# Two Mamba layers of 32 units each: two phases with their own set-up, or one phase of 64 units

## The reference, cut to what matters

```python
def _mamba_block(seq, ln_g, ln_b, in_w, conv_w, conv_b, xproj_w, dt_w, dt_b, A_log, Dp, out_w):
    h = (seq - mu) * jax.lax.rsqrt(var + EPS) * ln_g + ln_b          # over the 96 channels
    xs, z = jnp.split(h @ in_w, 2, axis=-1)                          # 192 each
    xc = silu(sum(conv_w[:, k] * xp[:, k:k + L, :] for k in range(4)) + conv_b)   # causal
    dbl = xc @ xproj_w                                               # 6 + 16 + 16
    delta = softplus(dbl[..., :6] @ dt_w + dt_b)
    dA = exp(delta[..., None] * A)                                   # A = -exp(A_log), 192 x 16
    dBx = delta[..., None] * Bm[:, :, None, :] * xc[..., None]
    hstates = scan of h[l] = dA[l] * h[l-1] + dBx[l]                 # l = 0 .. 4095
    y = (einsum('blds,bls->bld', hstates, Cm) + Dp * xc) * silu(z)
    return y @ out_w

for i in range(2):                                                   # the two layers
    seq = seq + _mamba_block(seq, <weights of layer i>)
```

## Time and profile before

| | |
|---|---|
| median of 3 runs | 7883.33 us (7870.8 to 7883.77) |
| the profiled execution | 7886.06 us, its span 7884.2 us |
| TensorE's granted clock, mean of full speed | 0.865 |
| busy share of the span: DVE, PE, POOL, ACT | 82%, 79%, 69%, 67% |
| `mamba_hs` scans on DVE, both layers | 1536, of 1271 ns mean |
| `mamba_prod` on POOL, both layers | 1536, 1929.6 us |
| Mamba layers, from the first instruction to the fusion's first one on DVE | about 3119 us |

### The profile page before, as it was taken

How to read it: one execution, slowest core, us unless ns; L and a number is a source line. 1 busy time by engine, 2 the same in 40 slices (tenths; PEclk the granted TensorE clock), 3 DMA queues, 4 the chain that set the end, 5 groups by cost and what they waited for, 6 DMA issues and landing times. The chain is left out here.

```text
span 7884.2 us, 105029 instructions
## 1 busy us (share of the span) xinstructions
PE 6253.2 (79%) x18336; PEld 2158.2 (27%) x18336; DVE 6471.5 (82%) x7496; ACT 5278.1 (67%) x10931; POOL 5467.5 (69%) x4288
## 2 busy tenths in 40 slices
PE   7888788678888885477888888888888777889786
PEld 2222222122222221122222222222222212478342
DVE  6999999869999998379999999999999995633636
ACT  6777777667777774366777777777777774322656
POOL 5888888768888886068888888888888893000516
PEclk8888988889888887688888999888888887998888
DMA  3444444344444444367777777777777774246322
GB/s 91 105 98 96 104 105 103 77 94 97 99 109 104 98 99 107 109 162 176 174 181 180 180 181 180 180 179 183 180 179 181 182 184 105 92 155 178 103 65 74
DMA packets 580429, 1050.78 MB, mean 133 GB/s; under 512 B 101719, under 2 KB 136812, under 8 KB 575180
## 3 DMA queue, kind: packets, MB, share of 16 engines
q1 hardware_dynamic: 580140, 1047.89, 54.7%
HBM read 858.09 MB, written 189.54 MB: 133 GB/s over the span
## 5 line engine op out<-in xcount | busy, mean ns | idle before, releaser
L1574 POOL TENSOR_TENSOR scan_prod<-scan_hs,scan_BC_rep 128x512 f32<-128x512 f32 x1536 | 1942.9, 1274 | 427.5 <-DVE scan_hs L1498 422.8
L597 POOL TENSOR_TENSOR mamba_prod<-mamba_hs,mamba_BC_rep 128x512 f32<-128x512 f32 x1536 | 1929.6, 1273 | 387.4 <-DVE mamba_hs L557 365.2
L557 DVE TENSOR_TENSOR_SCAN mamba_hs<-mamba_dA,mamba_carry,mamba_dbx 128x512 f32<-128x512 f32 x1152 | 1463.9, 1271 | 0.0
L1123 PE MATMUL scan_u_rep<-scan_du,scan_sel 96*128 96x512 f32 x1536 | 968.7, 716 | 472.4 <-DVE scan_hs L1498 471.8
L496 ACT ACTIVATE mamba_dA<-mamba_delta_rep,mamba_a_neg 128x512 f32<-128x512 f32 x1536 | 1091.0, 712 | 202.2 <-DVE mamba_hs L557 201.2
L1348 ACT ACTIVATE scan_dA<-scan_delta_rep,scan_a_neg 128x512 f32<-128x512 f32 x1536 | 1092.3, 712 | 90.9 <-DVE scan_hs L1498 80.4
L1498 DVE TENSOR_TENSOR_SCAN scan_hs<-scan_dA,scan_carry,scan_u_rep 128x512 f32<-128x512 f32 x768 | 976.0, 1271 | 158.6 <-ACT scan_carry L1328 153.9
L544 DVE TENSOR_TENSOR mamba_dbx<-mamba_u_rep,mamba_BC_rep 128x512 f32<-128x512 f32 x1152 | 788.0, 684 | 309.4 <-DMA mamba_BC_rep<-bc_units 131.9
L1498 DVE TENSOR_TENSOR_SCAN scan_hs<-scan_dA,scan_carry,scan_dbx_even 128x512 f32<-128x512 f32 x768 | 975.5, 1270 | 31.7 <-ACT scan_carry L1328 27.3
L315 PE MATMUL mamba_u_rep<-mamba_du,mamba_sel 96*128 96x512 f32 x768 | 483.4, 715 | 406.8 <-DVE mamba_hs L557 400.1
L1897 POOL TENSOR_TENSOR ffn_sq<-ffn_xm 96x512 f32<-96x512 f32 x64 | 66.3, 1036 | 954.7 <-DVE ffn_xm L1865 944.6
(11 more groups left out here) (283 smaller groups left out, 10476.9 us busy)
## 6 DMA issues: line engine op xcount, KB each, us to landing
scan_BC_rep<-proj_rows SPq DMA_DIRECT2D x1024, 256.0 KB, 6.4
scan_delta_rep<-proj_rows SPq DMA_DIRECT2D x1024, 192.0 KB, 3.5
mamba_BC_rep<-bc_units SPq DMA_DIRECT2D x256, 512.0 KB, 10.4
mamba_delta_rep<-delta_units SPq DMA_DIRECT2D x512, 192.0 KB, 3.6
proj_rows<-scan_dbc SPq DMA_DIRECT2D x256, 224.0 KB, 2.6
delta_units<-mamba_delta SPq DMA_DIRECT2D x128, 192.0 KB, 6.2
by_n<-fin_res SPq DMA_DIRECT2D x32, 768.0 KB, 3.2
fmid_src<-by_n SPq DMA_DIRECT2D x32, 768.0 KB, 5.0
```

Of the source, the lines that this page charges most:

```text
L557: nc.vector.tensor_tensor_scan(hs[:, s % RING_H], dA[:, s % RING_A], dbx_bank(s)[:], carry[:, bass.ds(at, 1)], op0=ALU.mult, op1=ALU.add). ...
L597: pool.tensor_tensor(prod[:, (G * u + s) % RING_P], hs[:, s % RING_H], BC_rep[:, u, QUADS + s % QUADS], ALU.mult).then_inc(s_prod, 1)
L1123: nc.tensor.matmul(u_rep[c][:], sel[:, c], du[:, k], start=True, stop=True).then_inc(s_rep_u, 1)
L1574: pool.tensor_tensor(prod[:, (G * k + s) % RING_P], hs[:, (G * k + s) % RING_H], BC_rep[:, k, 2 + s % 2], ALU.mult).then_inc(s_prod, 1)
```

## The change

`mamba_phase` is called once, with three arrays (`x_units`, `seq[0]`, `seq[1]`) and both layers' weights. Its units are numbered 0 to 63; unit 32 is the second layer's first. `bodies` now gives each unit the layers of the units from n - 1 to n + 3, and has two loops of 13 pairs (2 to 27 and 34 to 59) with straight code around: 0 and 1, 28 to 33, and 60 to 63. All steps take their weights from the layer of the unit they work on, so that units 30 and 31 prepare units 32 and 33 with layer 1's weights.

- Weights stand twice, as lists by layer. To save space the taps are loaded into `w_conv` and multiplied in place, A_log into `a_neg`, and the small `x_dt` and `w_dt` into rows of `hs`. Both sets are loaded at the start, the second right after the first two inputs; ACT and PE derive the second set after they have prepared unit 1, and DVE its taps before its first product.
- `carry` is a ring of 8 unit slots (and a ninth that takes what the first layer's last four units hand on, which nobody reads). At unit 28 DVE waits for its own last scan and clears the four slots in which units 32 to 35 begin.
- Units are loaded from and stored to the array of their layer.
- The barrier and the set-up between the layers are gone.

What it does to the order on the engines:

DVE, the kernel before, from the last scans of the first layer to the first product of the second (L525 to L534 set up constants and the taps).

The diff, cut to its core (every `lay` that is only passed on is left out):

```diff
-def mamba_phase(nc, name, x_in, x_out, bc_rows, delta_rows, w):
+def mamba_phase(nc, name, x_layers, bc_rows, delta_rows, weights):
...
+    NU = 2 * UNITS
+    SLOTS = 2 * B
...
+        w_in, w_conv, conv_b, dt_b, skip, ln_g, ln_b, w_proj, w_out, a_neg, skip_w = (
+            [p.sb(f"{what}{lay}", shape) for lay in range(2)]
...
+        x_dt, w_dt = ([hs[0:R, 2 * lay + v, 0:2 * C] for lay in range(2)] for v in range(2))
...
-        carry = p.sb("carry", [128, (UNITS + B) * G])
+        carry = p.sb("carry", [128, (SLOTS + 1) * G])
...
+            def at(n):
+                body(n, n % 2, [m // UNITS if 0 <= m < NU else None for m in (n - 1, n, n + 1, n + 2, n + 3)])
+
+            for n in range(2):
+                at(n)
+            for first, end, lay in ((2, UNITS - 4, 0), (UNITS + 2, NU - 4, 1)):
+                with eng.Fori(first // 2, end // 2) as i:
+                    body(2 * i, 0, [lay] * 5)
+                    body(2 * i + 1, 1, [lay] * 5)
+                for n in range(end, min(end + 6, NU)):
+                    at(n)
...
+            load_weights(0, s_w, ((sel, "sel"), (gather, "gather"), (ident, "ident")))
+            x_first = x_layers[0]
+            sp.dma_start(xin[:, 0], x_first[:, 0]).then_inc(s_xin[0], 16)
+            sp.dma_start(xin[:, 1], x_first[:, 1]).then_inc(s_xin[1], 16)
+            load_weights(1, s_w1, ())
...
+            pe.wait_ge(s_w1, 16 * NW1)
+            delta_weights(1)
+            pe.wait_ge(s_wconv1, 1)
+            pe.wait_ge(s_wd, 4)
+            pe.wait_ge(s_diag, 5)
             pe.wait_ge(s_du, 1)
...
+            def layer_weights(lay):
+                nc.scalar.activation(a_neg[lay][:], a_neg[lay][:], ACT.Exp).then_inc(s_aexp, 1)
+                act.wait_ge(s_aexp, lay + 1)
+                nc.scalar.mul(a_neg[lay][:], a_neg[lay][:], -1.0).then_inc(s_a, 1)
...
+            act.wait_ge(s_w1, 16 * NW1)
+            layer_weights(1)
             bodies(act, body)
...
+            conv_weights(0, s_wconv)
+            dve.wait_ge(s_w1, 16 * NW1)
+            conv_weights(1, s_wconv1)
...
+                at_first, = (dve.snap(v) for v in (n % SLOTS * G,))
+                if isinstance(n, int) and n == UNITS - B:
+                    dve.wait_ge(s_scan, G * n)
+                    nc.vector.memset(carry[:, UNITS % SLOTS * G:(UNITS % SLOTS + B) * G], 0.0).then_inc(s_zeroed, 1)
+                if isinstance(n, int) and n == UNITS:
+                    dve.wait_ge(s_zeroed, 1)
...
-                    at = G * n + s
+                    at = at_first + s
...
-    mamba_phase(nc, "mamba0", x_units, seq[0], bc_units, delta_units, w["mamba0"])
-    mamba_phase(nc, "mamba1", seq[0], seq[1], bc_units, delta_units, w["mamba1"])
+    mamba_phase(nc, "mamba", (x_units, *seq), bc_units, delta_units, (w["mamba0"], w["mamba1"]))
```

More of the change, by code:

```diff
@@ L225, in spread, with body @@
                 spread_delta(v, 1, landed)
-            def body(n, u, has_next, has_ahead):
-                load, last, read, done, landed = (sp.snap(v) for v in (n + 3, n - 1, n + 2, n + 2, 16 * n + 32))
-                now = sp.snap(n)
-                if not (isinstance(n, int) and n + 3 >= UNITS):
+            def body(n, u, lays):
+                prev, lay, nxt, _, after = lays
+                read, done, landed, now = (sp.snap(v) for v in (n + 2, n + 2, 16 * n + 32, n))
+                own, = (sp.snap(v) for v in (n - UNITS * lay,))
+                if after is not None:
+                    load = sp.snap(n + 3 - UNITS * after)
@@ L232, in body @@
                     wait(sp, s_mean, read)
-                    sp.dma_start(xin[:, 1 - u], x_in[:, bass.ds(load, 1)].rearrange("c a t -> c (a t)")
+                    sp.dma_start(xin[:, 1 - u], x_layers[after][:, bass.ds(load, 1)].rearrange("c a t -> c (a t)")
                                  ).then_inc(s_xin[1 - u], 16)
-                wait(sp, s_out, last)
-                sp.dma_start(xres[:, u], x_in[:, bass.ds(now, 1)].rearrange("c a t -> c (a t)")
+                if prev is not None:
+                    sp.wait_ge(s_out, now)
@@ L256, in _, with delta_weights @@
             pe.wait_ge(s_w, 16 * NW)
-            for half in range(2):
-                if half:
-                    pe.wait_ge(s_wd, 1)
-                nc.tensor.matmul(y[:, 0:2 * C], x_dt[:, half * C:half * C + C], w_dt[:],
-                                 start=True, stop=True).then_inc(s_wd_ps, 1)
-            pe.wait_ge(s_set, 4)
+            def delta_weights(lay):
+                for half in range(2):
+                    wait(pe, s_wd, 2 * lay + half)
+                    nc.tensor.matmul(y[:, 0:2 * C], x_dt[lay][:, half * C:half * C + C], w_dt[lay],
+                                     start=True, stop=True).then_inc(s_wd_ps, 1)
+            delta_weights(0)
+            pe.wait_ge(s_set, 3)
             pe.wait_ge(s_diag, 3)
@@ L309, in project_out @@
                 pe.wait_ge(s_yg, 2 * n + kh + 1)
-                mm = nc.tensor.matmul(out_ps[:], w_out[:, kh], ysk[:, kh], start=False, stop=(kh == 1))
+                mm = nc.tensor.matmul(out_ps[:], w_out[lay][:, kh], ysk[:, kh], start=False, stop=(kh == 1))
                 if kh == 1:
```

240 lines of the change are left out of this document (116 added, 124 removed).

## The result

| | before | changed |
|---|---|---|
| median of 4 runs each | 7882.11 us (7870.8 to 7883.77) | 7805.52 us (7796.01 to 7816.38) |
| the profiled execution | 7886.06 us, span 7884.2 us | 7796.01 us, span 7793.9 us |
| TensorE's granted clock, mean of full speed | 0.865 | 0.871 |

The changed kernel takes 0.9908 of the time (95% interval 0.9895 to 0.992), which is 63 to 83 us less. The forecast was 7810.

What follows compares the result with a forecast made beforehand. DVE was taken to bound both Mamba layers, so the gain was its idle time at the seam. 78.64 - 4.24 - 0.4 - 0.3 = 73.7 us off the median 7883.33 gave 7810 us, range 7796 to 7830.

Steps and rivals of the forecast that it cites:

- The gap closes: Seam between the Mamba layers: DVE's distance from last scan to next first scan falls from 80.41 to 1.77 us, 78.64 removed.
- The straight units: Units around the seam: units 30 and 31 now prepare later ones, at 45.80 us a unit; 4.24 us given back together.
- The clearing of carries: Unit 28: DVE waits for its own last scan, then clears 96 columns; 0.4 us lost, at most 1.27 for the wait.
- The start: Kernel start: the second layer's weights add SP issues and ACT work ahead of the first decay; 0.3 us, ends 0 and 2.6.
- The loops: Mamba loops: nothing removed, and the extra register instructions hide behind the scan before; 0 us.
- Units 30 to 33: Sign of being right, at the seam: these units take 44 to 47 us.
- DVE's busy time: Sign of being right: DVE is busy less than before, by under 1 us.
- looped steps longer than 1.8 us on average: Sign of being wrong, in the Mamba loops: DVE's product-and-scan steps average above 1.8 us.
- That the seam is dear: Rival: the six straight units at the seam run like the slowest unit, 7829 us; chance 0.08.
- That TensorE's clock falls without a pause: Rival, second layer: TensorE becomes the bound, the spread-matmul wait doubles and 55 us come back, 7865; chance 0.02.
- That the carry's address costs on every looped scan: Rival, looped units: 0.059 us per scan eats the gain, 0.1 us each makes it 7934; slower, chance 0.02.
- That the loop edges change: Rival, Mamba loops: DVE's stops at pass ends vanish, 7783, or come in all 26 passes, 7841; chance 0.05 for both.

Runs made afterwards that it cites:

- serial: The changed kernel with units 32 and 33 prepared after units 30 and 31 instead of under them; 7862.39 us, ratio to before 0.9975.
- again: The changed kernel run once more with no edit; 7802.67 us, ratio to before 0.9908.
- before_straight: The kernel before, still two phases, with all Mamba units in straight code; 7793.01 us, ratio to before 0.9898.
- loop4: The changed kernel with four units per pass of the Mamba loops instead of two; 7756.73 us, ratio to before 0.9848.
- straight: The changed kernel with all 64 Mamba units in straight code, no loops; 7719.84 us, ratio to before 0.9802.
- all_straight: The changed kernel with the Mamba units and the later selective-scan phase's units all in straight code; 7628.25 us, ratio to before 0.9689.

## Why the prediction was right

The time was 7805.5 us against 7810 forecast, and by the ratio 7883.33 x 0.9908 = 7810.8. The mechanism was the one predicted: the gap, by far the largest term, closed, and nothing else of that size moved. That the sum agrees to a few us is luck in part, since the measurement leaves 10 us to either side and the small terms did not come out as priced. Term by term:

1. **The gap closes, 78.64 us.** Exact, 80.41 to 1.77. `serial` adds what the prediction could not split: it named the drain, the weights and the chain of preparation as one, and by the runs they are 21 and 59 us.

2. **The straight units, 4.24 us given back: not borne out.** Units 28 to 33 take 266.78 us in the changed kernel (1373.61 to 1640.39) and 266.91 in `again`; the prediction had 6 x 45.80 = 274.8, against 270.5 for the same six units before. In these two profiles the term is thus 3.7 us gained. The 45.80 came from one pair of units in one trace, 28 and 29, and this pair differs from profile to profile, with or without the change: 88.58 us in the changed kernel, 88.45 in `before_straight`, but 91.43 in `loop4` and 91.57 in `straight`, like the 91.59 before. Over the eight profiles that have the overlap and delta first, the six units take 265.4 to 270.1 us, 44.2 to 45.0 a unit. Without loops they take 269.44 us joined (`straight`) and 268.34 not joined (`before_straight`, its gap reduced to one step), 1.1 us given back. So 45.80 was too high for a full unit, and the sign of the term stays open; in no pair of these profiles is it larger than some 5 us either way.

3. **The clearing of carries, 0.4 us:** 0.22. DVE's timeline at unit 28 of the changed kernel:
```profile
1371.62 1.27 DVE L597 TENSOR_TENSOR_SCAN mamba_hs<-mamba_dA,mamba_carry,mamba_u_rep 128x512 f32<-128x512 f32 x1
1372.97 0.14 DVE L584 MEMSET mamba_carry<- 128x96 f32 x1
1373.03 0.67 DVE L577 TENSOR_TENSOR mamba_dbx<-mamba_u_rep,mamba_BC_rep 128x512 f32<-128x512 f32 x1
1373.61 1.27 DVE L597 TENSOR_TENSOR_SCAN mamba_hs<-mamba_dA,mamba_carry,mamba_dbx 128x512 f32<-128x512 f32 x1
...
1640.39 1.27 DVE L597 TENSOR_TENSOR_SCAN mamba_hs<-mamba_dA,mamba_carry,mamba_dbx 128x512 f32<-128x512 f32 x1
```
The scans stand 1.99 us apart, not 1.77.

4. **The start, 0.3 us (0 to 2.6):** the first scan starts at 71.74 and 70.56 in the two profiles of the changed kernel, and at 69.30 to 71.61 in the eight others with one phase, against 70.21 before and 70.26 in `before_straight`. The mean of the ten is 70.9, 0.7 later. ACT and DVE at the start of the changed kernel:
```profile
63.18 0.21 ACT L400 ACTIVATE mamba_a_neg<-mamba_a_neg 128x24 f32<-128x24 f32 x1
...
65.94 0.33 ACT L408 ACTIVATE mamba_w_proj<-mamba_y 96x192 f32<-96x192 f32 x1 [0.65 <-PE mamba_y L264]
66.17 2.55 ACT L522 ACTIVATE mamba_dA<-mamba_delta_rep,mamba_a_neg 128x512 f32<-128x512 f32 x4
...
70.53 1.30 DVE L577 TENSOR_TENSOR mamba_dbx<-mamba_u_rep,mamba_BC_rep 128x512 f32<-128x512 f32 x2 [53.49 <-DMA mamba_BC_rep<-bc_units]
```
The second layer's set-up holds ACT for 3 us ahead of its first decay, and DVE's first product still waits for B and C until 70.53: the cover held, as said.

5. **The loops, 0 us.** The late starts behind jumps sum to 50.4 us before and 46.0 after, 24 jumps in each, so nothing worth counting. The rest of the layers' shortening, some 11 us beyond term 2 in the profiled executions, is not explained. Most of it lies ahead of the twelfth scans, where DVE's excess over 1.77 us is 95.3 us before, 82.2 and 80.9 in the two profiles of the changed kernel, and 87.6 in `serial`, whose loops are the same; without loops it is 50.5 not joined, and 54.2 and 63.5 joined. Profiles of the same Mamba code thus differ by 9 us there. Both profiles of the changed kernel were the fastest of their four runs, and the ratio over all runs needs no such term. Whether the change has a part in it stays open.

The signs. The scans at the seam stand 1.77 us apart, the first scan starts before 73 us, the clock is 0.88. Units 30 to 33 take 44.71, 43.75, 43.75 and 45.99 us, two of them just under the 44 to 47 given. DVE's busy time is 0.7 us higher, not lower (6472.2 against 6471.5). One sign of being wrong was badly set: looped steps longer than 1.8 us on average. With the stops in, the average was 1.95 and 1.93 us before, in the two loops, and is 1.94 and 1.92 now; the 1.77 is that of a step without a stop.

The rivals. That the seam is dear (7829) fell with the 44.5 us a unit of term 2. That TensorE's clock falls without a pause: the granted clock was 0.88 in both layers, against 0.87 before with the pause. That the carry's address costs on every looped scan: the median of DVE's looped steps is 1.77 us as before. That the loop edges change: they did not, but my reading of them was wrong. I took the 12 waits called "issue" as the 12 passes out of 26 that have a stop, and so thought it a matter of chance or place. Each taken jump has one, 24 of 24; half of them bore PE's name, as two stops do above. The rival's bounds, 7783 and 7841, were therefore no bounds: the stops were all there already, and in these runs went only with the jumps.

## What to carry to other kernels

When two phases do the same work on different data, the gain of joining them is the idle time of the bound engine at the seam, and here three quarters of it came only because the next part's first units are prepared under the last ones of the old: joining alone gave 20 us of 72. Look at the bound engine's first instruction behind each backward jump, by time between like instructions and not by the names in the list of waits: in the Mamba layers, with passes of 93 us, the jumps cost 1% of this kernel, and a loop body twice as long got back over half of that. Then look by position in the unit before you put a gain down to jumps: in the next phase the same edit gained as much, but by a table load that changed places with a wait. Before removing a wait, look at what the engine would reach next: with PE's wait gone, the transfer behind it took back a good part of the gain.

## What the runs showed of the hardware that I had not expected

- In the Mamba layers a taken backward jump costs 3.3 to 3.5 us (83 us for 24, 46 us for 14), of which 1.9 us are DVE's own late start; DVE is on time where a loop is entered or left. In the selective-scan phase, with a jump every 49 us, DVE's unit starts changed by 3 us in sum when 55 jumps went. Why the two differ is not shown.
- A load of ACT's activation table takes 1.28 us. Ahead of ACT's wait for PE it was hidden; behind it, in the loops of the selective-scan phase, DVE stopped 2.8 to 3.1 us in most units where it otherwise stopped 1.2.
- The instruction queues' traffic follows neither the jumps nor the time: 2.89 MB before, 3.38 in the changed kernel, 3.80 in `loop4`, 3.37 in `straight` and in `before_straight`, 5.13 in `all_straight`.
- Four transfers of 512 KB put ahead of four of 192 KB on one queue cost 136 us in 7612: the median time from issue to landing of the 192 KB ones went from 3.7 to 7.5 us.
